# A graph-network kernel on one core: attention sums copied as two whole banks, GpSimd's library called once in the first layer, and the first masked product put behind the second block's scores

## The reference

```python
x = _layernorm(x + _L0_gnn_ref(x, adj, L0_gnn_W, L0_gnn_b))     # adj @ (x W) + b
x = _layernorm(x + _L1_gnn_ref(x, adj, L1_gnn_W))               # mean over the neighbours
x = _layernorm(x + _L2_gnn_ref(x, ..., adj))                    # two rounds of the layer below
x = _layernorm(x + _L3_gnn_ref(x, adj, L3_gnn_weight, L3_gnn_bias))
```

```python
structural = _safe_norm(x @ W, axis=1)
att = jax.nn.softmax(Q @ edge_feat.T * scale * H, axis=1)
att_scores = att.mean(axis=0)                          # a sum over each column of att
comp_scores = jax.nn.softmax((0.5 * structural + 0.5 * att_scores) / TAU)
comp_mask = comp_scores >= th_comp
...
edge_scores = jax.nn.softmax(cos * H / TAU, axis=1)    # cos: of the masked, normed rows
edge_mask = (edge_scores >= th_edge) & comp_mask[:, None]
H_pruned = H * edge_mask
```

## Time and profile before

| | |
|---|---|
| three runs, median | 2486.67 us (2482.66 to 2487.47) |
| the profiled execution, device time | 2481.99 us |
| its span in the trace | 2480.2 us |
| PE busy | 2061.4 us (83%) |
| DVE busy | 1767.8 us (71%) |
| ACT busy | 784.4 us (32%) |
| POOL busy | 4.1 us |
| DMA, mean over the span | 336 GB/s |

### The profile page before, as it was taken

The page is one execution under the profiler, slowest core; times in us unless marked ns, Lnnn a source line. Parts: engine busy times, 40 slices in busy tenths (PEclk is TensorE's granted clock), DMA queues, the critical chain, the costliest instruction groups (busy, mean ns, idle before and its releaser), DMA issues. The chain is left out here.

```text
span 2480.2 us, 36406 instructions
## 1 busy us (share of the span) xinstructions
PE 2061.4 (83%) x15632; PEld 729.8 (29%) x15632; DVE 1767.8 (71%) x2037; ACT 784.4 (32%) x992; POOL 4.1 (0%) x16
## 2 busy tenths in 40 slices
PE   6788959889966766689999979986677779996898
PEld 2224234223321111133334323332111123333333
DVE  7875983068869998865553228869999975554898
ACT  0001001046633333311110016653333311111897
POOL 0000000000000000000000000000000000000000
PEclk9999989999988888799999999988888889998999
DMA  9976989989929999977778989947999997773796
GB/s 381 421 321 252 428 337 402 429 324 378 347 102 408 415 410 404 375 255 277 277 267 344 428 339 379 376 168 302 418 413 410 379 348 267 275 274 155 290 421 257
DMA packets 123484, 834.15 MB, mean 336 GB/s; under 512 B 8512, under 2 KB 10560, under 8 KB 76608
## 3 DMA queue, kind: packets, MB, share of 16 engines
q1 hardware_dynamic: 121136, 829.48, 83.7%
q10 hardware_dynamic: 2192, 2.40, 0.3%
HBM read 695.54 MB, written 136.31 MB: 335 GB/s over the span
## 5 line engine op out<-in xcount | busy, mean ns | idle before, releaser
L884 ACT ACTIVATE stream<-stream,negmax 128x4096 f32<-128x4096 f32 x128 | 475.3, 3713 | 530.8 <-DVE negmax L878 530.8
L840 PE MATMUL ps<-edgeT,node_twice 64*128 64x512 f32 x1024 | 299.4, 710 | 187.6 <-DVE mx L873 187.6
L873 DVE CUSTOM_DVE_ANT_0 stream<-ps,stream 128x1024 f32<-128x1024 f32 x352 | 415.0, 1220 | 54.8 <-PE ps L840 32.9
L426 PE MATMUL ps<-stream,stage 128*64 128x512 f32 x1792 | 401.8, 598 | 57.0 <-DMA stream<-in_adjT 30.7
L840 PE MATMUL ps<-edgeT,query_twice 64*128 64x512 f32 x1024 | 249.5, 619 | 6.2 <-DVE edgeT L905 4.0
L1158 PE MATMUL ps<-stream,xw 32*64 32x512 f32 x4096 | 224.9, 589 | 1.2 <-ACT xw L1242 0.6
L426 PEld LDWEIGHTS ps<-stream,stage 128*64 128x64 f32 x1792 | 126.4, 137 | 324.4 <-issue 249.3
L840 PEld LDWEIGHTS ps<-edgeT,node_twice 64*128 64x128 f32 x1024 | 99.6, 211 | 371.0 <-DVE mx L873 266.6
L855 PE MATMUL ps<-stream,ones 128*1 128x512 f32 x1024 | 172.3, 807 | 11.3 <-DVE stream L1198 11.3
L1198 DVE SCALAR_TENSOR_TENSOR stream<-stream,cut 128x4096 f32<-128x4096 f32 x40 | 179.4, 4485 | 1.4
L1377 DVE SCALAR_TENSOR_TENSOR query_twice<-stream,query_twice 128x512 bf16<-128x512 f32 x256 | 154.7, 681 | 4.6 <-ACT query_twice L1355 4.5
(11 more groups left out here) (192 smaller groups left out, 1691.7 us busy)
## 6 DMA issues: line engine op xcount, KB each, us to landing
stream<-in_adj SPq DMA_DIRECT2D x140, 2048.0 KB, 13.5
stream<-in_adjT SPq DMA_DIRECT2D x74, 2048.0 KB, 13.2
pruned<-stream SPq DMA_DIRECT2D x64, 2048.0 KB, 10.5
spare<-in_adj SPq DMA_DIRECT2D x26, 2048.0 KB, 10.0
spare<-pruned SPq DMA_DIRECT2D x22, 2048.0 KB, 11.2
query_twice<-pruned SPq DMA_DIRECT2D x22, 2048.0 KB, 11.2
node_twice<-pruned SPq DMA_DIRECT2D x20, 2048.0 KB, 11.5
query_twice<-in_adj SPq DMA_DIRECT2D x12, 2048.0 KB, 15.5
```

The lines of the kernel that those rows point to most:

```text
L426: last = nc.tensor.matmul(ps[F * h:F * h + F, bank + b, :], stage[:, t.k % SL, :], half_bank(src, b, h), start=False, stop=False, skip_gro ...
L840: last = nc.tensor.matmul(ps[:, 2 * slot + h, :], stationary[F * h:F * h + F, rows_n], bank_of(edgeT[F * h:F * h + F, :], c), start=True, ...
L873: nc.vector.tensor_tensor_reduce(out=prod[s][:, cols], in0=ps[:, 2 * slot:2 * slot + 2, :].rearrange("p a b -> p (a b)"), in1=block_in[:, ...
L884: nc.scalar.activation(prod[s], prod[s], ACT.Exp, bias=negmax[:, s:s + 1], accum_out=zsum[:, s:s + 1]).then_inc(exp_done, 1)
```

## The change

The diff is the whole change. It has these parts:

- `column_sums_begin` writes zeros to all 128 partitions of banks 6 and 7, with one 128x512 matmul for each bank, in place of four one-row matmuls for each.
- The hand-over copies all 128 partitions of bank 6 on VectorE and of bank 7 on ScalarE, one 128x512 copy each, in place of two 1x1024 copies each. TensorE waits for VectorE's copy ahead of its first four matmuls and for ScalarE's ahead of the last four.
- In `l0` GpSimd runs one `partition_all_reduce` of zeros behind its constants.
- In the prune pass product 0 moves behind scores 1.

```diff
-        def rows_to_columns(bank):
+        def rows_to_columns(bank, before=lambda half: None):
...
             for m in range(8):
+                if m % 4 == 0:
+                    before(m // 4)
                 last = nc.tensor.matmul(in_slots[:, m // 4, m % 4], rows[:, P * m:P * m + P], ident[:, 0::32],
...
             @block.gpsimd
             def _(pool):
+                nc.gpsimd.memset(gl["gsum"][:, :], 0.0).then_inc(reduce_zero, 1)
                 nc.gpsimd.memset(ident[:, :], 0.0).then_inc(ident_zero, 1)
...
+                pool.wait_ge(reduce_zero, 1)
+                nc.gpsimd.partition_all_reduce(gl["gsumall"][:, :], gl["gsum"][:, :], P,
+                                               bass.bass_isa.ReduceOp.add).then_inc(reduce_ready, 1)
+                pool.wait_ge(reduce_ready, 1)
...
             for half in range(2):
-                for g in range(4):
-                    nc.tensor.matmul(ps[32 * g:32 * g + 1, 6 + half, :], zeros_b[:, 0:1], zeros_b[:, :],
-                                     start=True, stop=False, skip_group_check=True)
+                nc.tensor.matmul(ps[:, 6 + half, :], zeros_b[:, 0:P], zeros_b[:, :],
+                                 start=True, stop=False, skip_group_check=True)
+
+        def take_all_rows(copy, half):
+
+            return copy(rows[:, BANK * half:BANK * half + BANK], ps[:, 6 + half, :])
...
-                    take_rows(nc.scalar.copy, 6, (0, 1), rows_taken)
+                    take_all_rows(nc.scalar.copy, 1).then_inc(high_taken, 1)
...
-                    pe.wait_ge(rows_taken, 4)
-                    rows_to_columns(0).then_inc(att_ready, 1)
+                    rows_to_columns(0, lambda half: pe.wait_ge((rows_taken, high_taken)[half], 1))\
+                        .then_inc(att_ready, 1)
...
-                    take_rows(v.tensor_copy, 6, (2, 3), rows_taken)
+                    take_all_rows(v.tensor_copy, 0).then_inc(rows_taken, 1)
...
-                        if t.k == 0:
-                            prune(t)
-                        if t.k >= 2:
+                        if t.k >= 1:
                             prune(t.back(1))
```

More of the change, by code:

```diff
@@ L606, in build @@
             order_zero, order_made = sem("order_zero"), sem("order_made")
+            reduce_zero, reduce_ready = sem("reduce_zero"), sem("reduce_ready")
             after = tmp[:, 0:2, :].rearrange("p a f -> p (a f)")
@@ L962, in build @@
                 rows_taken, att_ready, chain = sem("rows_taken"), sem("att_ready"), sem("dve_step")
+                high_taken = sem("high_rows_taken")
                 comp_ready, mask_ready, masked = sem("comp_ready"), sem("mask_ready"), sem("nodes_masked")
```

## The result

The changed kernel takes 2466.17 us (median of 6 runs, 2460.09 to 2469.78), the kernel before 2483.24 us beside it (6 runs, 2482.66 to 2487.47). The ratio is 0.992, with a 95% interval of 0.9905 to 0.9935: 16 to 24 us less, and 20 by its middle. Two further sets of runs of the same change gave 0.9936 (0.9921 to 0.995) and 0.9927 (0.9911 to 0.9944), which is 16 and 18 us. The forecast was 15.0 us less and 2470. The direction and the places were right, and the size was too small.

The account below looks back on a forecast made before the run. VectorE was taken to bound the prune pass at its head, transfers most of its length; in the hand-over all wait for all. Gains of 5.17 + 1.79 + 8.06 = 15.0 us from 2484.7 gave 2469.7, say 2470; range 2464 to 2477.

Parts of the forecast that it names:

- The copies: Hand-over: 128x512 copies let TensorE begin at 700.27 in place of 702.07; 1.79 us taken a round.
- The eight matmuls stay as they are: Hand-over: TensorE's matmuls keep 3.19 and 3.57 us; any shortening from less idle time before them left at nothing.
- Rival 3: VectorE keeps its whole lead, 4.93 us a round, and the eight matmuls run faster: 17 to 18 us, 2467; chance 0.07.
- The library call: First hand-over: the all-reduce's wait behind VectorE's maximum falls from 3.47 us, gaining 3.38; nothing in the second round.
- takes about 10 us: `l0`: library load and reduce end near 10.2 + 10 = 20 us, while `l1` opens at 184.07; no engine waits.
- The moved product: Prune pass: scores 1 cover ScalarE's exponential; 4.03 us a round, 8.06 in all, bounds 2.1 and 4.93.
- The zero matmuls: Two full ones replace eight one-row ones; gain 0.2 us a phase at best, cost 0.4 at worst; taken as 0.
- `l0`'s costs: One memset ahead of the constants, covered by VectorE's idle time, at most 0.28 us uncovered; 0 taken, 0.3 allowed.
- The sum: Whole kernel: 5.17 + 1.79 + 8.06 = 15.0 us less, forecast 2469.7, say 2470.
- The choice of a base between the two levels of the runs: Executions lie in pairs near 2482.3 and 2487; their mean, 2484.7, was the base for the forecast.

Follow-up runs that it names:

- e4: The change with the product order of the kernel before put back, so all of it but the moved product; ratio 0.997 (0.9956 to 0.9984).
- e7: The change with prune-pass loads cut to half a block, so the pruned matrix isn't the reference's; passes of 301.76 and 302.36 us.
- e8: The change with half-block loads in the prune pass and the old order of the products; passes of 306.56 and 306.57 us.
- e9: The change with whole-bank copies behind the prune pass too; ratio 0.9906 (0.9893 to 0.9919) to the kernel before, median 2460.34 us.
- e1: The change without the all-reduce in `l0` and with the old order of the products; ratio 0.9988 (0.9978 to 0.9999) to the kernel before.
- e12: The kernel before, with block 4's load held until the masked operand's first part is made; first-round all-reduce begins 0.13 us behind the maximum.
- e3: The kernel before with only the first product moved behind the second block's scores; ratio 0.9967 (0.9956 to 0.9978).

## Why the prediction was right or wrong

**The copies: right.** "TensorE's first half ... can begin at 700.27 in place of 702.07": it begins 0.75 us behind the copies in place of 2.54, in both rounds of every profile with these copies.

**"The eight matmuls stay as they are ... whether that makes them shorter I leave at nothing": the step that failed.** They are on the chain in full and took 1.95 us where the clock still stood at its upper level, against 3.19 and 3.57. In the seven profiles with both early edits and no added matmuls (the change three times, e4, e7, e8, e9) they took 1.95 us in every first round, and in the second 1.95 twice, 2.20 to 2.40 four times and 3.58 once. The rows were at hand: the earlier trace rows had two lengths for the same eight matmuls, which is itself a sign of the clock. Rival 3 had it as a possibility with a chance of 0.07, which was too low. It is worth 1.2 us in the first round and about 1.2 on average in the second.

**The library call: right in place and size, wrong in its working.** The wait fell from 3.47 to 0.10 us, and no second load came. That the edits hang together was right, too (e1, e4). But "takes about 10 us" is no fixed time of the load: it took 6.26 to 8.61 us in `l0`, and in e12, with the block's transfer held back, at most 7.0 in the hand-over. What the load moves over the DMA queues no run shows: in its wait in `l0` (10.11 to 16.93 us of the change) the queue of the earlier trace rows has no packet. The 0 that the forecast has for it in `l0` is borne out only by the time up to the first hand-over (below).

**The moved product: right.** Predicted 4.03 us a round, measured 4.1 on average. The reading that the pass is VectorE's at its head and the transfers' after it fits: with light loads VectorE has no unnamed wait left in its passes, where the change has 18.3 us of them in its first, and the lead that stands at the fourth block (4.80 and 4.19 us) is there at the end (4.80 and 4.21). How much of the lead full transfers take is known only to some 0.3 us. The profile of the change by itself would have led to rival 3's 4.9.

**The zero matmuls and `l0`'s costs: nothing**, as taken: the zero matmuls are busy for 2.4 us in all before and after, and up to the first hand-over's copies the ten profiles with the new call take 697.1 to 701.3 us, the four without it 699.2 to 703.0.

**The sum.** First hand-over 10.1 against 16.56, 6.5 us (predicted 5.17); second 3.0 as the mean over those seven profiles, 10.5 against 13.5 (predicted 1.79); passes 2 x 4.1 (predicted 2 x 4.03): 17.7 us against 15.0. With e3's hand-over of 15.47 as the old one, where the load ended 1 us sooner, it is 16.6. The three measurements of the whole, 16, 18 and 20 us, have both in their intervals. In the profiled pair the four edited pieces are 19.4 us shorter, and the stretches that no edit touches are 3.2 us longer, which makes the 16.2 us between the two spans. What is left of the 20 us of the first measurement is not found in any piece; the scatter of single executions is large enough for it. The choice of a base between the two levels of the runs was sound: the more runs of before there were, the more they filled the space between 2478 and 2490.

## What to carry to other kernels

A short chain in which all engines wait for each other is worth more than its busy times say: each piece counts in full (the copies took 1.8 us off the second hand-over in e1), and the pieces can hide each other (beside the load the same copies gained nothing in the first, 15.54 against 15.47 us), so undo them one by one and then in pairs before you book a gain to one of them. When the same instructions have two lengths in one trace, look at the granted clock beside them (here 1.95 us at 1.00, 3.57 at 0.50); an edit that lets them start earlier may change their length too. And in a pass that the transfers bind, an edit at its head need not give the whole lead that it wins for the engine (here 4.1 of 4.9 us on average): average over many passes, since one profile may show all of it. Last, look at the stages behind an edit too, since a gain that one stage shows may be missing from the whole.

## What the runs showed of the hardware that I had not expected

- A GpSimd library load took 6.26 to 8.61 us in `l0`, at a DMA share of 0.99 to 1.02, and at most 7.0 us in the hand-over with no other transfer (e12, one profile); it ended 9.0 to 10.0 us behind the start of the copies where a 2 MB transfer was issued at the same time. The cause of the difference is open.
- The eight 128x128 matmuls took 1.95 us at a granted clock of 1.00 and 3.57 at 0.50, and the same program met either in different executions.
- With matmuls of zeros in its waits TensorE had 1.95 us in four cases of four, and the whole kernel was no faster for it within what was measured. In both profiles with them the last stretch of the kernel took 479 to 480 us, against 471 to 476 in the twelve others, at a granted clock of 0.93 and 0.94 against 0.95 to 0.96; that the one brings the other is not shown.
